# Another order of TensorE's work inside a cross-attention group of a decoder layer

## The reference

```
x = x + attn(layernorm(x))          # causal, 16 heads of 64
x = x + xattn(layernorm(x), ctx)    # differential cross attention, ctx is 2 x 154 x 128
x = x + ffn(layernorm(x))           # 128 -> 512, conv over 3 tokens, silu, 512 -> 128, 8-bit inputs

# xattn: 16 heads of 8; each head's query and key are two halves of 4
logits_s = q_s @ k_s.T * 0.5        # s = 1, 2; 32 softmaxes over 154 keys in each batch
a = softmax(logits_1) - lam * softmax(logits_2)
out = (a @ v) * 0.8
```

## Time and profile before

| what | us |
|---|---|
| median of 3 runs | 355.93 (352.65 to 364.46) |
| the profiled execution | 353.06 |
| its span | 351.2 |
| group 0 starts (score 0) | 204.76 |
| starts of groups 1 to 7 | 216.69, 231.69, 243.12, 252.96, 262.77, 277.31, 289.35 |
| last value tiles of group 7 | 304.20 |

### The profile page before, as it was taken

How to read it: one execution, slowest core, us unless ns; L and a number is a source line. 1 busy time by engine, 2 the same in 40 slices (tenths; PEclk the granted TensorE clock), 3 DMA queues, 4 the chain that set the end, 5 groups by cost and what they waited for, 6 DMA issues and landing times.

```text
span 351.2 us, 6679 instructions
## 1 busy us (share of the span) xinstructions
PE 300.8 (86%) x2486; PEld 184.1 (52%) x2486; DVE 225.9 (64%) x504; ACT 207.2 (59%) x512; POOL 120.6 (34%) x194
## 2 busy tenths in 40 slices
PE   1698699889999999789999989979997887788694
PEld 0465466556666696566667643434443342255472
DVE  3844666886666616876664697747778764068654
ACT  2475567667777716867776247547776457326254
POOL 3624637784477806743644003033240000000000
PEclk9998999999999999999999996889999897699698
DMA  7800000000000000000000000000000000000001
GB/s 283 309 3 3 0 3 1 2 2 0 3 2 3 2 0 3 2 2 0 2 2 4 0 2 0 0 1 2 0 3 0 2 1 0 0 2 0 0 24 39
DMA packets 4835, 6.19 MB, mean 18 GB/s; under 512 B 833, under 2 KB 3649, under 8 KB 4674
## 3 DMA queue, kind: packets, MB, share of 16 engines
q1 hardware_dynamic: 4514, 5.42, 4.3%
q10 hardware_dynamic: 288, 0.33, 0.3%
HBM read 5.23 MB, written 0.52 MB: 16 GB/s over the span
## 4 chain that ended last, share of the span: by engine, by line
PE 56%; DVE 19%; ACT 14%; issue 6%; DMA 2%; POOL 1%; SPq 0%; ACTq 0%; DVEq 0%
PE bank L605 52%; ACT pT L416 4%; ACT pr L416 3%; DVE nmax L1137 3%; PE bank L678 3%; DMA x_sb<-in_x 2%; DVE qk L1194 2%; ACT pT L522 2%; DVE nmax L1143 2%; DVE pT L1165 1%; DVE qk L1201 1%; DVE onT L1318 1%; DVE stats L1074 1%; POOL pr L300 1%; DVE rx L1312 1%
## 5 line engine op out<-in xcount | busy, mean ns | idle before, releaser
L522 ACT ACTIVATE pT<-bank 128x512 f32<-128x512 f32 (+1 forms) x80 | 45.1, 600 | 39.0 <-PE bank L605 38.1
L1194 DVE TENSOR_REDUCE qk<-bank 128x4 fp32r<-128x616 f32 x64 | 48.8, 796 | 24.1 <-PE bank L605 23.8
L300 POOL TENSOR_SCALAR pr<-pr,pinv 128x384 f32<-128x384 f32 (+2 forms) x96 | 46.1, 500 | 46.4 <-DVE pinv L1151 46.4
L416 ACT ACTIVATE pr<-bank,nmax 128x384 f32<-128x384 f32 (+2 forms) x96 | 44.6, 481 | 18.3 <-DVE nmax L1143 18.3
L605 PE MATMUL bank<-qs 64*128 64x512 f32 (+3 forms) x256 | 49.1, 465 | 4.5 <-ACT pT L416 4.5
L605 PE MATMUL bank<-pT,v_sb 128*64 128x128 f32 (+2 forms) x320 | 38.4, 385 | 0.0
L310 POOL TENSOR_TENSOR km<-kb_,con 128x1232 fp32r<-128x1232 f32 x8 | 18.0, 2245 | 55.2 <-PE bank L605 53.7
L1165 DVE COPY pT<-bank 128x512 f32<-128x512 f32 (+1 forms) x32 | 30.4, 952 | 6.9 <-PE bank L678 6.8
L605 PE MATMUL bank<-km,qk 64*128 64x308 f32 x128 | 32.2, 382 | 2.3 <-DVE qk L1194 1.0
L416 ACT ACTIVATE pT<-bank,nmax 128x512 f32<-128x512 f32 x32 | 21.7, 683 | 20.4 <-DVE nmax L1137 20.4
L605 PE MATMUL bank<-qk,km 64*128 64x512 f32 x64 | 29.4, 509 | 4.0 <-ACT pT L522 3.6
(11 more groups left out here) (162 smaller groups left out, 582.2 us busy)
## 6 DMA issues: line engine op xcount, KB each, us to landing
pT<-in_wqk SPq DMA_DIRECT2D x1, 1024.0 KB, 6.3
cw_sb<-in_cw SPq DMA_DIRECT2D x1, 768.0 KB, 8.7
x_sb<-in_x SPq DMA_DIRECT2D x2, 256.0 KB, 5.4
pT<-in_wv SPq DMA_DIRECT2D x1, 512.0 KB, 7.0
wo_sb<-in_wo SPq DMA_DIRECT2D x1, 512.0 KB, 7.2
out<-x_sb SPq DMA_DIRECT2D x8, 64.0 KB, 1.6
onT<-in_consts ACTq DMA_DIRECT2D x1, 256.0 KB, 6.4
pT<-in_xwk SPq DMA_DIRECT2D x1, 256.0 KB, 7.6
```

Of the source, the lines that this page charges most:

```text
L300: nc.gpsimd.tensor_scalar(d, d, pinv[:, t, a:a + 1], 1.0, ALU.mult, ALU.mult).then_inc(norm_done, 1)
L416: nc.scalar.activation(prob[r][:, a, at:at + w], bank[:, SP[k % 2] + a, at:at + w], ACT.Exp, bias=nmax[:, t, a:a + 1], accum_out=psum[:, t ...
L522: nc.scalar.activation(px[rows, i, :], bank[rows, (ST0, ST1)[i % 2], :], ACT.Exp, scale=SD ** -0.5).then_inc(xexp_done, 1)
L1194: nc.vector.tensor_reduce(m, s_in, AX.X, ALU.max, negate=True).then_inc(round_done, 1)
```

## The change

Inside a group, on TensorE: the projection `stack_queries(G + 2)` goes ahead of the second value tiles `cross_weighted(G - 1, 1)`; the rest keys `cross_weighted_rest(G)` (and the turned normalisation of group 1) go from behind score 4 to behind score 3; the turned maxima `turn_cross_max(G + 1)` go from behind score 8 to behind score 7, and the first value tiles `cross_weighted(G, 0)` from behind score 6 to right behind them. `cross_out(0)` stays behind score 4. On ScalarE: `query_parts(G + 2)` goes from behind exponential 2 to behind exponential 1, ahead of `copy_sums(G - 1)`; the copy of the turned normalisation in group 1 goes from behind exponential 6 to behind exponential 4. VectorE, GpSimd and the DMA queues keep their order. No instruction is added or removed.

```diff
@@ -558,18 +558,19 @@
 
             for G in range(B * NG):
                 cross_exps(G, range(0, 2))
+                if G + 2 < B * NG:
+                    query_parts(G + 2)
                 if G >= 1:
                     copy_sums(G - 1)
                 cross_exps(G, range(2, 3))
-                if G + 2 < B * NG:
-                    query_parts(G + 2)
                 if G == 6:
                     turned_att(0)
-                cross_exps(G, range(3, 7))
+                cross_exps(G, range(3, 5))
+                if G == 1:
+                    turned_norm(1, 4, PJ0)
+                cross_exps(G, range(5, 7))
                 if G == 0:
                     root_of_variance(1, 4)
-                if G == 1:
-                    turned_norm(1, 4, PJ0)
                 cross_exps(G, range(7, 8))
                 if G == B * NG - 1:
                     act.wait_ge(zero_done, 3)
@@ -1006,30 +1007,30 @@
                     if 6 <= i < 8 and G + 2 < B * NG:
                         cross_max(G + 2, i - 6, first)
                     if i == 1:
+                        if G + 2 < B * NG:
+                            stack_queries(G + 2)
                         if G >= 1:
                             cross_weighted(G - 1, 1)
-                        if G + 2 < B * NG:
-                            stack_queries(G + 2)
                         if G == 6:
                             pe.wait_ge(qb1_done, 7)
                             turn_att(0)
                     if G == 5 and i in SUMS_AFTER_ROUND:
                         turn_sums(0, SUMS_AFTER_ROUND[i])
-                    if i == 4:
+                    if i == 3:
                         if G == 1:
                             pe.wait_ge(xq_act, 8)
                             turn_norm(1, 4, PJ0)
-                        if G == 6:
-                            cross_out(0)
                         cross_weighted_rest(G)
+                    if i == 4 and G == 6:
+                        cross_out(0)
                     if G == B * NG - 1 and i == 5:
                         turn_ints(0)
-                    if i == 6:
-                        cross_weighted(G, 0)
-                    if i == 8 and G + 1 < B * NG:
+                    if i == 7:
                         if G == 6:
                             pe.wait_ge(xo_done, 1)
-                        turn_cross_max(G + 1, reduced)
+                        if G + 1 < B * NG:
+                            turn_cross_max(G + 1, reduced)
+                        cross_weighted(G, 0)
 
             pe.wait_ge(wcs, 4)
             pe.wait_ge(w2q_done, 1)
```

## The result

The changed kernel took 364.79 us (median of 4 runs, 363.2 to 365.15), and the kernel before 354.29 beside it: a ratio of **1.0337, 95% interval 1.029 to 1.0385**, slower by 3.4% where no change within 2% was the likeliest forecast and 363 the end of its range. The profiled execution took 365.05 us, 12.0 more than that of the kernel before.

What follows compares the result with a forecast made beforehand. TensorE was taken to bound the kernel, busy 86% of the span. Group terms 0 + 4.4 + 0.5 + 0.9 - 1.2 = +4.6 us on 353.06 gave 357.7 us; own range 354 to 361, 8 in 10 349.5 to 363.

Steps and rivals of the forecast that it cites:

- Nothing behind the cross stage changes: Stages after the cross stage: they start with what group 7's last value tiles leave, priced at no change.
- four groups at +1.1: Groups 1 to 4 of the cross stage: each goes from 9.84 to 10.94 us, 4.4 us for the four.
- group 5 at +0.5: Group 5, VectorE's: value tiles between turn and score 8 make the boundary's chain cost +0.5 us.
- the tail at 0: The stretch behind the cross stage's last group: forecast to change by 0 us.
- Rival B: TensorE's clock falls from the new idle: about 1 us more in five groups, 362.7 us; chance 16%.
- The direct term: Cross stage: the new order's own price summed over the groups, +4.6 us.
- The boundary: Between groups, before score 0: a wait of 0.7 to 0.9 us for exponential 8 replaces one of 0.45.
- The middle: Score 4 to round 1: 2.99 us, TensorE standing about 1 us before round 1; expected to decide.
- The rest keys: Ahead of score 4: 0.99 us of work covers its wait for exponential 2; waiting for `copy_sums` at worst 0.15.
- The projection: Ahead of the second value tiles: exponential 2 some 0.3 us later; uncovered, score 4 would cost the same 0.2.
- group 7: Last group: two ScalarE operations leave the way to the last value tiles, 0.9 us, plus 0.3 at score 4: -1.2.
- Group 0: First group: the earlier sum helps and the boundary takes it back, 0 us, between -0.9 and +0.5.

Runs made afterwards that it cites:

- e4: Changed kernel with VectorE's query rows behind the maximum of round 5 instead of round 6; ratio 1.032 to the kernel before.
- e7: Kernel before with only the projection ahead of the second value tiles and its output taken out ahead of the copy of sums; ratio 1.000.
- e3: Kernel before with only the rest keys (and group 1's turned normalisation with its copy) moved, to behind score 3; ratio 1.000.
- e2: Kernel before with only the turned maxima moved behind score 7 and the first value tiles behind them; ratio 1.032.
- e9: Changed kernel with the first value tiles back behind score 6, the turned maxima staying behind score 7; ratio 1.024 to the kernel before.
- e5: Kernel before with the whole new order in group 5 alone; ratio 1.011.
- e8: Kernel before with the whole new order in groups 0 and 7 alone; ratio 1.013, interval 0.994 to 1.033.
- e14: Kernel before with one added TensorE wait for exponential 5, between score 5 and round 7, in groups 1 to 4; ratio 1.006.
- e13: Kernel before with score 7 of groups 1 to 4 issued five times, adding TensorE work and no idle; ratio 1.008.
- e1: Changed kernel with 6 repeated score matmuls a group in groups 1 to 5, placed where TensorE waits; ratio 1.050 to the kernel before.
- e11: Kernel before with one added TensorE wait for exponential 7, between score 7 and round 1, in groups 1 to 4; runs 357.3, 358.4, 364.5, 366.5 us.
- e10: Changed kernel with the first value tiles one place later, behind score 8, the turn staying at 7; ratio 1.054 to the kernel before.

## Why the prediction was wrong

**The step that failed** is the sum's last one: "Nothing behind the cross stage changes" and, with it, that the terms were priced at the clock of the profile before (four groups at +1.1, group 5 at +0.5, the tail at 0). The clock was a rival with 16% and +5 us, and not a term. It took 5 to 6 us, and 4.6 + 5.8 is the 10.4 measured between the means. Rival B's own figure, 362.7 us, stood nearest, and at 364.8 it was still short: it counted a 1 us price in some five groups, where group 5 alone lost 5.1 us beyond its forecast and the stage behind 1.6. The forecast's own range was also mis-added: its stated bounds give 353.6 to 359.8 us, not 354 to 361.

**The direct term held**, as closely as the line can tell. +4.6 us forecast, 4.6 above the line measured (3.8 at like clocks, up to 6.2 by the flatter line); that the figures are equal is partly luck, since group 1 gave 1.1 us less than forecast. The group at full clock comes out at 10.9 us from e4's and the changed kernel's stretches, as forecast. Its parts, each alone and at full clock: projection +0.06 (e7), rest keys +0.38 (e3), turned maxima with the first value tiles +0.57 (e2), together 1.0 of the 1.1.

**Inside it, point by point.** *The boundary* was right: L522 in place of L1201. The way from score 8 to score 0 is 1.27 us at full clock (252.10 to 253.37 in e4), where 1.19 was forecast. *The middle* had the right chain and length, 2.89 for 2.99, with one reader left out: round 0 of group G + 2 reads the query rows, so most of the idle time shows there, ahead of round 0, and the maximum of round 7 sets only what is left at round 1. It was not the deciding step: e4 took 0.58 us of it out and e9 gave the cover back, and both stayed 3.8 and 4.2 us above the line. *The rest keys* were priced as a small gain at score 4; alone they cost 0.38, by the two waits that e3 shows. *The projection* was said to leave at most today's 0.2 us of waiting at score 4 if nothing covered it; uncovered, in e7, it is 0.41. *Group 5* and *group 7*: +0.5 by the order held in e5 (0.5 above the line), and -1.2 was measured as -1.2, and as -1.1 at like clocks in e8 and e14. *Group 0* gained by its clock alone (e8).

**What the evidence for the clock was worth.** The prediction read group 5 at 1.00 with TensorE busy 78% as evidence against rival B. In the kernel before that group held its clock; in the changed kernel it ran at 0.58, and in e13, in the old order, at 0.60 (18.56 us against 14.54). One group in one execution said nothing on how often it would hold. The three runs of before shown at the start, 352.65 to 364.46 us, were the better evidence: such a spread in one program on one core could have been read as a term that comes and goes. The Trainium skill (TensorE: Matmul & The Clock Gate, A second HAM failure mode) says of another kernel that frequent short idles between groups of matmuls made the clock swing between its levels. The changed kernel's clock does swing, from 1.00 in group 0 to 0.58 in group 5 and 0.82 in group 6; but e1 and e4, which fill or remove some of the idle, don't undo it.

**Open.** Why the changed kernel has a low clock in every run. That idle raises the chance of it is argued and not shown: e14 against e13 and the split of e11 lean that way, while e1 speaks against idle as the whole cause, and so does e8, whose clock is 0.919 with hardly any price of its own (0.4 above the line); only 15 of the 67 runs of before are at 0.925 or less. e2's edit alone is enough for the low clock (0.900), but no run here gives the single wait or the pattern that does it, and whether it is the shift of later work in time, with no idle added, was tested only by e13. Nor did any version beat the kernel before; e7 ties with it.

## What to carry to other kernels

Where the granted clock of a profile is uneven, plot the times of many runs of one kernel over their mean clock before explaining any difference: here the line (1.9 us per hundredth) splits a 10.4 us loss into order and clock, and keeps a group that was merely entered at a low clock from being blamed on its order. When work is moved off a place, price each reader of the chain that it used to cover, not only the last one, and count the wait for a freed bank next to the wait for data: removing an operation from between a score and its reuse uncovers the exponential. And in a group that is nearly full of TensorE work, a move that "covers" one wait pays for it with the cover of another; three small ones together cost 11%.

## What the runs showed of the hardware

- One program on one core, unchanged, ran from 349.98 to 361.41 us over 67 runs on four chips, with a mean granted clock from 0.958 to 0.902; 190.7 us per unit of clock. On one of the chips alone, 14 runs went from 350.67 to 361.41 us.
- The clock can stay at the lower level through dense work: group 6 of e1 ran 18.52 us at 0.50 with TensorE busy for 17.27 of it, while group 2 of the kernel before, busy 10.81 of 11.43, had a mean of 0.85 and the next groups 1.00.
- A VectorE operation on 128x512 float32 took 1.44 us instead of 0.74 while GpSimd did a float32 addition of 128x512 (e10). The same operation of group 4 took 1.42 to 1.83 us in e1, e2, e3, e4 and e9.
